# Counting the repair signals on GpSimd, and ScalarE's relus ahead of one-hots and of V's second half

## The reference

```python
mask = A != 0
scores = jnp.where(mask, -jnp.arange(N), -inf)
vals, idx = jax.lax.top_k(scores, 25)
feats = where(valid, x[idx], -inf);  agg = feats.max(axis=2)
agg = where(degree <= 25, maximum(agg, 0.0), agg)
h = concatenate([X, agg], axis=-1)
out = relu(einsum('bnf,fo->bno', h, W) + b)
x = layernorm(x + out)
```

## Time and profile before

| | us |
|---|---|
| median of 3 runs | 627.07 |
| lowest and highest | 624.03 and 629.14 |
| the profiled execution's own time | 624.25 |
| its span, first to last instruction | 622.4 |
| busy in the span: PE, DVE | 501.3 (81%), 534.3 (86%) |
| ACT, POOL | 394.6 (63%), 290.4 (47%) |

### The profile page before, as it was taken

One profiled execution on the slowest core, in us unless ns is written; L12 is line 12 of the kernel. 1 busy time (PEld: TensorE's weight loads), 2 busy tenths in 40 slices (PEclk: granted clock), 3 DMA queues, 4 the chain that ended last, 5 costly groups with the idle time before them and its releaser, 6 DMA issues.

```text
span 622.4 us, 14481 instructions
## 1 busy us (share of the span) xinstructions
PE 501.3 (81%) x4480; PEld 341.9 (55%) x4544; DVE 534.3 (86%) x973; ACT 394.6 (63%) x751; POOL 290.4 (47%) x462
## 2 busy tenths in 40 slices
PE   1366997889968996889974999679987999779982
PEld 0124675566654675456752666555764567555762
DVE  4656999899898998899995998998898999998884
ACT  3361577448965688557864588665886478545744
POOL 2643365246633655146733356335552467336610
PEclk9997999899998999799997999998999999899996
DMA  8982336353434647345534445355544463021102
GB/s 244 224 221 72 102 98 129 98 153 96 134 95 137 151 115 125 106 130 143 132 97 112 133 107 137 86 141 137 135 124 120 116 141 59 18 57 36 46 10 70
DMA packets 91815, 71.38 MB, mean 115 GB/s; under 512 B 63651, under 2 KB 80294, under 8 KB 91686
## 3 DMA queue, kind: packets, MB, share of 16 engines
q1 hardware_dynamic: 85286, 56.77, 35.6%
q0 software_dynamic: 6400, 13.12, 8.4%
HBM read 50.99 MB, written 4.19 MB: 89 GB/s over the span
## 4 chain that ended last, share of the span: by engine, by line
PE 30%; DVE 22%; issue 14%; ACT 12%; DVEq 8%; DMA 7%; another core or an unknown queue 3%; POOL 1%; SPq 1%; POOLq 1%; ACTq 0%
PE pair L1037 25%; DVE part L776 11%; DMA adj_sb<-in_adj 3%; ACT row_work L712 3%; DMA g_feat<-in_x,g_idx 3%; DVE hot L771 3%; ACT mask L586 3%; DVEq L846 3%; DVEq L915 2%; ACT distance L629 2%; ACT hot L636 2%; DVE g_feat L849 2%; PE misc L1082 1%; DVE g_val L817 1%
## 5 line engine op out<-in xcount | busy, mean ns | idle before, releaser
L1037 PE MATMUL pair<-hot,x_part 128*128 128x128 bf16 (+3 forms) x3120 | 416.6, 281 | 66.0 <-DVE part L776 33.8
L1037 PEld LDWEIGHTS pair<-hot,x_part 128*128 128x128 bf16 x3120 | 239.0, 99 | 176.1 <-issue 64.0
L776 DVE TENSOR_REDUCE part<-pair 128x128 f32<-128x1024 f32 (+1 forms) x256 | 279.8, 1099 | 47.2 <-PE pair L1037 45.9
L484 POOL DMA_INDIRECT g_feat<-in_x,g_idx x200 | 192.8, 964 | 112.5 <-issue 96.0
L521 POOL TENSOR_TENSOR y_sb<-relu_sb,x_sb 128x128 f32<-128x128 f32 x64 | 32.8, 512 | 194.1 <-ACT relu_sb L647 193.8
L593 ACT ACTIVATE V<-p_V 128x512 bf16<-128x512 f32 x98 | 58.0, 592 | 93.4 <-remote 71.7
L621 ACT ACTIVATE hot<-V,first_bias 128x1024 bf16<-128x1024 bf16 x56 | 64.1, 1145 | 52.8 <-PE pair L1037 52.8
L771 DVE TENSOR_SCALAR hot<-V 128x1024 bf16<-128x1024 bf16 x224 | 84.3, 397 | 0.0
L586 ACT ACTIVATE mask<-adj_sb 128x1024 bf16<-128x1024 uint32 x56 | 58.8, 1050 | 20.5 <-DMA adj_sb<-in_adj 20.5
L636 ACT ACTIVATE hot<-distance,one 128x1024 bf16<-128x1024 bf16 x56 | 64.0, 1143 | 0.2
L629 ACT ACTIVATE distance<-V,second_bias 128x1024 bf16<-128x1024 bf16 x56 | 63.7, 1137 | 0.0
(11 more groups left out here) (88 smaller groups left out, 396.6 us busy)
## 6 DMA issues: line engine op xcount, KB each, us to landing
adj_sb<-in_adj SPq DMA_DIRECT2D x56, 512.0 KB
g_adj<-in_adj SPq DMA_DIRECT2D x8, 512.0 KB, 4.4
x_sb<-in_x SPq DMA_DIRECT2D x8, 512.0 KB, 3.9
out<-y_sb SPq DMA_DIRECT2D x7, 512.0 KB, 5.1
g_feat<-in_x,g_idx POOLq DMA_INDIRECT x200
maskT<-mask SPq DMA_TRANSPOSE x56
out<-y_sb SPq DMA_DIRECT2D x1, 448.0 KB, 3.0
w_sb<-in_W SPq DMA_DIRECT2D x1, 128.0 KB, 6.3
```

The lines of the kernel that those rows point to most:

```text
L484: pool.indirect_dma_start(out=g_feat[w][:, k, :], out_offset=None, in_=x_rows, in_offset=bass.IndirectOffsetOnAxis(ap=g_idx[w][:, k:k + 1] ...
L776: dve.tensor_reduce(part[:, par(q, s), :, p], slots_of(q, s, p).rearrange("f k i -> f i k"), AX.X, ALU.max).then_inc(s_used, 1)
L1037: last = pe.matmul(dst, x_part[:, q, part_no, kb], one_hot, start=(first and part_no == 0), stop=(final and part_no == PARTS - 1))
```

## The change

In a tile without repair GpSimd now counts up six more semaphores (eight in all), TensorE none, and VectorE only the one that it waits for itself. GpSimd's branch becomes two nested ones. In ScalarE's order the relu of tile s-1 moves from behind the second half of V to right behind the mask, ahead of `copy_xt`, the means, the squares and V's second half; the relus of tile 0 (in tile 1) and of tile 7 (in tile 2) move ahead of the first rank's one-hots.

```diff
@@ GpSimd, redo
-                with pool.If(lv == LEVELS):
-                    pool.dma_start(g_adj[1][:, :], adj_tiles[bass.ds(2 * NT * i + NT * q + s, 1)]
...
-                    pool.sem_inc(s_fg, 1)
+                with pool.If(lv > 0):
+                    with pool.If(lv == LEVELS):
+                        pool.dma_start(g_adj[1][:, :], adj_tiles[bass.ds(2 * NT * i + NT * q + s, 1)]
...
+                        pool.sem_inc(s_fg, 1)
+                    with pool.Else():
+                        pool.sem_inc(s_fadj, 1)
+                        pool.sem_inc(s_fg, 1)
                 with pool.Else():
+                    pool.sem_inc(s_xpair, EXTRA)
+                    pool.sem_inc(s_ft, 1)
+                    pool.sem_inc(s_hotx, 1)
+                    pool.sem_inc(s_xused, EXTRA)
+                    pool.sem_inc(s_fidx, 1)
+                    pool.sem_inc(s_fagg, 1)
                     pool.sem_inc(s_fadj, 1)
                     pool.sem_inc(s_fg, 1)
@@ ScalarE, step
-                    if nxt:
-                        first_rank(*nxt)
-                        second_distance(*nxt)
                     if s == 1 and not is_first(i, q):
                         relu(pi, pq, 0)
                     if s == 2 and not is_first(i, q):
                         relu(pi, pq, MT)
+                    if nxt:
+                        first_rank(*nxt)
+                        second_distance(*nxt)
                     if to_rank:
                         copy_V(*to_rank, 0)
                     if nxt:
                         second_rank(*nxt)
                     if to_mask:
                         make_mask(*to_mask)
+                    if s > 1:
+                        relu(i, q, s - 1)
                     if s in TURNS:
                         copy_xt(i, q, TURNS[s])
...
                     if to_rank:
                         copy_V(*to_rank, 1)
-                    if s > 1:
-                        relu(i, q, s - 1)
@@ VectorE, end of a tile
                     with dve.Else():
-                        dve.sem_inc(s_hotx, 1)
-                        dve.sem_inc(s_xused, EXTRA)
                         dve.sem_inc(s_xdone, 1)
-                        dve.sem_inc(s_fidx, 1)
-                        dve.sem_inc(s_fagg, 1)
@@ TensorE, end of a tile
                             pe.wait_ge(s_xdone, m + 1)
-                    with pe.Else():
-                        pe.sem_inc(s_xpair, EXTRA)
-                        pe.sem_inc(s_ft, 1)
```

More of the change, by code:

```diff
@@ L501, in redo @@
                 lv = pool.value_load(level[0:1, q, s - 1:s], min_val=0, max_val=LEVELS)
-                with pool.If(lv == LEVELS):
-                    pool.dma_start(g_adj[1][:, :], adj_tiles[bass.ds(2 * NT * i + NT * q + s, 1)]
-                                   .rearrange("a p n -> p (a n)")).then_inc(s_fdma, 16)
-                    before = pool.snap(redone, min_val=0, max_val=MAIN * 16 * (K + 1))
-                    pool.wait_ge(s_fdma, before + 16)
-                    pool.sem_inc(s_fadj, 1)
-                    wait(s_fidx, m + 1)
-                    gather(1, s_fdma, range(K))
-                    pool.wait_ge(s_fdma, before + 16 * (K + 1))
-                    pool.reg_add(redone, redone, 16 * (K + 1))
-                    pool.sem_inc(s_fg, 1)
-                with pool.Else():
+                with pool.If(lv > 0):
+                    with pool.If(lv == LEVELS):
+                        pool.dma_start(g_adj[1][:, :], adj_tiles[bass.ds(2 * NT * i + NT * q + s, 1)]
+                                       .rearrange("a p n -> p (a n)")).then_inc(s_fdma, 16)
+                        before = pool.snap(redone, min_val=0, max_val=MAIN * 16 * (K + 1))
+                        pool.wait_ge(s_fdma, before + 16)
+                        pool.sem_inc(s_fadj, 1)
+                        wait(s_fidx, m + 1)
+                        gather(1, s_fdma, range(K))
+                        pool.wait_ge(s_fdma, before + 16 * (K + 1))
+                        pool.reg_add(redone, redone, 16 * (K + 1))
+                        pool.sem_inc(s_fg, 1)
+                    with pool.Else():
+                        pool.sem_inc(s_fadj, 1)
+                        pool.sem_inc(s_fg, 1)
+                with pool.Else():
+                    pool.sem_inc(s_xpair, EXTRA)
[4 more added lines that the diff above has]
+                    pool.sem_inc(s_fagg, 1)
                     pool.sem_inc(s_fadj, 1)
```

## The result

The changed kernel takes **598.58 us** (median, 597.36 to 601.36) where the kernel before takes 625.55 us (622.15 to 629.14): ratio 0.9574, 95% interval 0.9507 to 0.9642. 607.6 was forecast, 599.0 to 619.0; the time lies 0.4 us under the range. Two later measurements gave less, and both of their times lie inside the range: 602.98 us beside 623.64 (0.9680, 0.9632 to 0.9728) and 602.44 beside 622.95 (0.9654, 0.9611 to 0.9698). The profiled execution took 601.36 us, span 599.6, mean granted clock 0.972 where it was 0.956.

A forecast was written before the change was run, and what follows sets the result against it. VectorE (86% busy) and TensorE (81%) were taken to bound it, each waiting for the other in different stages. Terms 7.2 + 6.7 + 4.2 = 18.1 us off 624.25 gave 606.2; half of 2.8 added made 607.6, range 599 to 619.

The forecast's parts named there:

- the gathered rows: Tile 7 of seven batches: early relus let GpSimd gather sooner, so VectorE's DMA wait goes; 6.7 us, bounds 0 and 6.7.
- the turn: Change of batch: relu of tile 6 early brings TensorE 1.37 us forward at seven turns; 4.2 us, bounds 0 and 9.6.
- the clock: Rival, chance 0.07: shorter idle at turns spares low-clock stretches, 1.7 us at four or five turns; 8 us more, 599.6.
- TensorE's two increments: Tile boundaries where TensorE leads, 24 in all: removing the pair saves 0.30 us each; 7.2 us, bounds 0 and 9.6.
- VectorE's four increments: After most tiles hidden under the last reduce of 1.23 us; open only at turns, 0.4 us for the four.
- The rule on queues: TensorE's 64-place queue would cover control work, making the 7.2 term 0; the prediction followed the profile row instead.
- TensorE's weight of this is nil: Tile 4: squares and V's second half, delayed behind the early relu, still end about 0.8 us before V can start.
- the second kind: Two turns where VectorE's first reduce waits 0.90 us for its own issue: 0.4 each from the four removed increments.
- the first kind: Two turns where VectorE's first reduce waits 1.23 us for TensorE: 1.0 us saved at each.
- The relus of tiles 0 and 7: Moved ahead of one-hots in tiles 1 and 2: nothing, since covered; otherwise up to 0.27 for each of 14, 3.8 us.
- GpSimd's increments: Six per tile at 0.1 us, 0.6 us a tile: nothing on the path, as 2.6 us remain where 1.7 is needed.
- The relu holds ScalarE: Rival, chance 0.03: in tiles 2 to 5 the relu's wait delays V's second half; 28 us lost, 634.

The follow-up runs named there:

- dve_sems_again: Kernel before with only VectorE's four increments moved to GpSimd, TensorE keeping its two, ScalarE's order old: 618.61 us beside 624.22, ratio 0.9920.
- relu_1to5: Kernel before with only the relus of tiles 1 to 5 moved ahead of V's second half, increments unchanged: 617.4 us beside 624.22, ratio 0.9892.
- relu_6: Kernel before with only the relu of tile 6 moved ahead of V's second half in tile 7: 621.55 us beside 623.54, ratio 0.998.
- before_again: The kernel before, unaltered, run again for its trace: 626.15 us in one execution, span 624.3.
- pe_sems_again: Kernel before with only TensorE's two increments moved to GpSimd, VectorE keeping its five: 618.69 us beside 623.54, ratio 0.9921.
- sems_only: Kernel before with all six increments moved to GpSimd, ScalarE's order old, in the slow first session: 671.45 us beside 675.83, ratio 0.9884.

## Why the prediction missed by 0.4 us

The sign and the order of size came out, and so did the term of the gathered rows; of the three terms of the sum two were mis-sized, in opposite directions. The step that failed, and that puts the time below the range, is the turn: it was summed only up to the first reduce of tile 1, at 4.2 us, and the clock was put at nothing in the sum. The three traces of the changed kernel have 2.9 to 3.4 us there and 2.0 to 3.3 more up to the second reduce, 5.0 to 6.3 in all (6.0 to 7.3 against the trace that the prediction was read from).

Of the 9.0 us between 607.6 and 598.58, 4.5 are in the sum: the reduces' starts differ by 22.6 us between the two profiled executions, not 18.1. 1.4 are the margin added on top (half of 2.8, in the wrong direction), 2.8 that the profiled execution of the changed kernel was the slowest of its four (601.36 to 598.58), and 0.3 lies outside the reduces. The 4.5 by place: 3.1 at the turns, 1.3 at the gathered rows (8.0 up to tile 7, not 6.7), 1.2 in the rest of tile 1 and in tile 7, less 1.1 from tile 1's last reduce to tile 5's (6.1, not 7.2). That the miss is a miss by 0.4 us is partly chance: the next two measurements of the same kernel lie inside the range.

Term by term:

- *TensorE's two increments* (7.2 forecast). Alone they gave 4.9 us. The price of about 0.3 a pair was right (their two starts are 0.2 apart and together 0.24 to 0.40 us go from tile 1 to tile 2), the count of three boundaries a batch was not: where the clock was 1.00, removing them shortened the boundary of tiles 1 and 2 and, by 0.18 to 0.30, tile 4, but not tile 3 or the boundary before it, except in the last batch. That VectorE can follow was argued from the sum of two idle times; only at two of three places did it.
- *VectorE's four increments* (nothing outside the turns). They are worth 5.0 us alone: 0.36 to 0.41 at three turns that can be compared, as forecast for their kind, and up to 0.7 in the rest of tile 1 (batches 2 and 8), which was not. The step "after most tiles they run under the last reduce" holds from tile 1's end to tile 5: nothing over 0.1 us at undisturbed places. Why tile 1 gains is not shown. The 1.6 us that the summed table would give dve_sems_again from tile 1 to tile 2 are, but for 0.1, the repaired tile of the first batch, which met no low clock there.
- *The rule on queues.* The Trainium skill (Advanced Engine Details and Errata, "Sequencer Loop" and "Engine Queue Depths") lets engine instructions be queued while control work runs, by which this work would have been covered. The run with two more increments, 11.3 us slower, contradicts that for this kernel.
- *The relus of tiles 1 to 6 and the gathered rows* (6.7). relu_1to5 alone took the wait away, and where the clock was 1.00 the stretch up to tile 7 is 0.9 to 1.2 us shorter a batch, seven times: the size is right too. Two steps were not: GpSimd still waits for the relu of tile 3, and "TensorE's weight of this is nil" fails, since with the relus early tile 4 takes 0.25 to 0.34 us longer in six batches (tile 3 0.25 less). That takes back in tile 4 what TensorE's increments give there. The cause of it is not shown.
- *The turn* (4.2). Up to the first reduce the size was near (2.9 to 3.4, or 3.7 to 4.3 against the trace it was read from), its parts were not all right. The two turns of the second kind gave the 0.4 of VectorE's increments, as forecast. The two of the first kind (the first and the third) were given 1.0 each, because TensorE would come 1.37 us earlier, from a row of 1.23 us that was read where the mean clock was 0.82. At full clock the third turn waits 0.90, relu_6 leaves it there, and VectorE's increments alone bring 0.37, which is all that comes. Of the two turns put at 0 one gave 0.06 and the other 0.67, and the loop's turn, put at 1.37, gave 0.3 to 1.1.
- *The clock*, a rival with 0.07, came true in part beside the forecast, not in its place. The second reduce's gain is nearly all this: in before_again it came 2.3 to 2.9 us after the first at three turns and 1.5 to 1.6 at the others, in the three traces after the change 1.53 to 1.67 at all turns but two (1.93 and 2.99). By the mean clock, 0.956 of 622.4 us and 0.972 of 599.6 us, TensorE spent about 55 us at 1.2 GHz before (0.044 x 622.4 / 0.5) and 34 after; the later traces give 51, and 34 and 41. Most of that difference is not at the turns: relu_1to5 alone comes to 38, the relu of tile 6 alone to 56. That the shorter idle time spared the stretch at a turn is the reading that fits; no run held the idle time and changed the clock alone, so the cause stays open.
- *The relus of tiles 0 and 7* (nothing forecast, 3.8 at worst): nothing, with and without the rest.
- *GpSimd's increments* (nothing on the path; 0.6 us a tile): 0.09 each, hidden, with about 2.5 us of margin left for the gathers.
- *The relu holds ScalarE* did not come: V's second half still waits, 0.75 us. What the early relus did cost is the quarter of a us in tile 4.

## What to carry to other kernels

Price a sequencer's increment from start to start, and then ask at each place which engine's own stream comes last: a wait that the profile puts down to another engine can be the waiting engine's own increments, as at the turns here. Compare the parts of a change place by place where the clock is the same, since sums over a run mix in stretches of low clock: by the sums of its trace pe_sems_again seems to gain 6.6 us from tile 1's last reduce to tile 5's, near the 7.2 forecast, while by its time TensorE's increments are worth 4.9. When summing what a turn gains, go on past the first waiting instruction until a reduce comes that would have waited anyway, and give the clock a term of its own in the sum where the row of a low stretch stands behind an idle time.

## What the runs showed of the hardware

The kernel before took 675.83 us in one session, on another chip, and 623 to 627 us in all others. There the same program was 8% slower, its parts ranked otherwise, and their traces have waits of up to 10.1 us before a reduce (sems_only) that the view can put down only to a remote release. Compare only what shares a session. An increment's row says 51 ns on TensorE, 21 on VectorE, 17 on GpSimd, while from start to start they take about 0.15 to 0.2, 0.1 and 0.09 us.
